# Layer norm by one VectorE instruction per pixel column, and the second stage's loop written out

## The reference, cut to what matters

```python
hidden = einsum('oc,bchw->bohw', w_hidden, x)            # 32 -> 192 channels
hidden = depthwise_3x3(hidden, w_dw)
q, k, v = split(hidden, 3, axis=1)                       # 64 channels each
out = irfft2(rfft2(patches_8x8(q)) * rfft2(patches_8x8(k)))
mu, var = out.mean(axis=1), out.var(axis=1)              # over the 64 channels, per pixel
out_norm = (out - mu) / sqrt(var + 1e-05) * norm_w + norm_b
return einsum('oc,bchw->bohw', w_out, v * out_norm)
x = x + that(group_norm(x))
```

## Time and profile before

| | us |
|---|---|
| median of 3 runs | 2822.24 |
| the profiled execution | 2816.64 |
| its span, first to last instruction | 2814.8 |
| TensorE matmul busy | 2501.0 (89%) |
| TensorE weight load busy | 1660.3 (59%) |
| VectorE busy | 1651.3 (59%) |
| ScalarE busy | 1439.9 (51%) |
| GpSimd busy | 466.5 (17%) |

### The profile page before, as it was taken

How to read it: one execution, slowest core, us unless ns; L and a number is a source line. 1 busy time by engine, 2 the same in 40 slices (tenths; PEclk the granted TensorE clock), 3 DMA queues, 4 the chain that set the end, 5 groups by cost and what they waited for, 6 DMA issues and landing times.

```text
span 2814.8 us, 95766 instructions
## 1 busy us (share of the span) xinstructions
PE 2501.0 (89%) x40199; PEld 1660.3 (59%) x40199; DVE 1651.3 (59%) x4058; ACT 1439.9 (51%) x2381; POOL 466.5 (17%) x322
## 2 busy tenths in 40 slices
PE   7888888699898999898989998999899989999998
PEld 3333333466666666666666666666666666666665
DVE  4666666455555555555555555555555555555565
ACT  3555656555555555554555555545555554455552
POOL 1000000012121212121212121212121212121221
PEclk9988989799999999999999999999999999999999
DMA  6688978622222222222222222222222222222222
GB/s 128 174 228 213 233 203 214 162 59 66 64 64 63 61 61 65 61 60 61 66 62 66 64 67 61 62 61 65 62 66 64 65 62 60 59 62 61 66 56 46
DMA packets 60403, 249.11 MB, mean 88 GB/s; under 512 B 12393, under 2 KB 12658, under 8 KB 53714
## 3 DMA queue, kind: packets, MB, share of 16 engines
q1 hardware_dynamic: 59954, 242.50, 35.2%
HBM read 140.74 MB, written 101.72 MB: 86 GB/s over the span
## 4 chain that ended last, share of the span: by engine, by line
PE 59%; DVE 11%; issue 6%; ACT 3%; DVEq 0%; SPq 0%; ACTq 0%; DMA 0%
PE bank L654 16%; PE bank L577 12%; PE bank L670 9%; PE bank L637 7%; PE bank L590 6%; PE bank L558 6%; PE bank L599 4%; ACT arena L820 3%; DVE arena L1122 2%; DVE arena L1134 2%; DVE arena L1099 2%; DVE arena L1109 2%; DVE arena L1141 2%; DVE arena L1129 1%; ACT arena L865 0%
## 5 line engine op out<-in xcount | busy, mean ns | idle before, releaser
L441 POOL TENSOR_TENSOR arena<-arena 128x8 f32<-128x8 f32 x256 | 442.3, 1728 | 1827.6 <-DVE arena L1115 1817.5
L811 ACT ACTIVATE arena<-bank 100x512 f32<-100x512 f32 x1024 | 614.8, 628 | 227.4 <-PE bank L558 209.8
L577 PE MATMUL bank<-arena 128*64 128x512 f16 x4608 | 711.9, 400 | 7.6 <-issue 4.3
L1199 DVE TENSOR_TENSOR arena<-bank,arena 128x512 f32<-128x512 f32 x512 | 354.3, 692 | 438.4 <-PE bank L654 412.5
L558 PEld LDWEIGHTS bank<-arena 128*36 128x36 f16 (+1 forms) x8192 | 334.1, 106 | 423.2 <-issue 126.9
L558 PE MATMUL bank<-arena 128*36 128x128 f16 (+1 forms) x8192 | 406.7, 224 | 170.3 <-DVE arena L1099 127.2
L654 PE MATMUL bank<-arena 100*64 100x128 f32 x8192 | 510.0, 274 | 7.6 <-DVE arena L1199 7.6
L654 PEld LDWEIGHTS bank<-arena 100*64 100x64 f32 x8192 | 455.7, 136 | 45.4 <-issue 37.3
L512 PE MATMUL bank<-arena 32*32 32x508 f32 (+1 forms) x9216 | 386.8, 654 | 52.6 <-issue 37.7
L820 ACT ACTIVATE arena<-bank,arena 128x256 f32<-128x256 f32 x512 | 261.6, 561 | 172.0 <-PE bank L590 169.4
L1134 DVE TENSOR_TENSOR arena<-arena,bank 128x512 f32<-128x512 f32 x256 | 175.9, 687 | 286.3 <-ACT arena L820 284.8
(11 more groups left out here) (112 smaller groups left out, 1587.0 us busy)
## 6 DMA issues: line engine op xcount, KB each, us to landing
arena<-xn_d SPq DMA_DIRECT2D x128, 536.2 KB, 8.1
xn_d<-arena SPq DMA_DIRECT2D x130, 260.0 KB, 4.5
x_d<-arena SPq DMA_DIRECT2D x64, 512.0 KB, 8.3
arena<-x_d SPq DMA_DIRECT2D x128, 256.0 KB, 4.7
out<-arena SPq DMA_DIRECT2D x128, 256.0 KB, 5.3
arena<-x_in SPq DMA_DIRECT2D x32, 544.0 KB, 9.9
arena<-x_in SPq DMA_DIRECT2D x32, 528.0 KB, 9.7
arena<-spectra_in SPq DMA_DIRECT2D x1, 1152.0 KB
```

The source lines that it names most:

```text
L441: pool.tensor_tensor(tiny["rstd"][:, slot], tiny["var_eps"][:, slot], powers, ALU.pow).then_inc(s_root, 1)
L577: mm = pe.matmul(v_banks[chunk % 3][64 * s:64 * s + 64, :], v_w[:, 64 * tap:64 * tap + 64], at(xs[half], row * WP + 32 * k + dx, [32 * WP, ...
L811: act.activation(h_rows[0:WIN, :, first:first + 4], banks[g % ring][0:WIN, :].rearrange("p (i c) -> p c i", i=4), ACT.Copy).then_inc(s_h_r ...
L1199: dve.tensor_tensor(parts(prod[m % 4][:, 512 * second:512 * second + 512]), parts(k_banks[n % 3]), q_sb[m % 2][:, 256 * second:256 * secon ...
```

## The change

Two things are done.

The first is the layer norm. `centre` and `scale` (one instruction of 512 elements each per piece, the second waiting for the first) and the copy of the means go. `normalise` stands for them: 8 tensor_scalar instructions per piece, one for each pixel column of 64 channels, which subtract the mean and multiply by the root, both read as a scalar per partition, the mean straight from the statistics. With it VectorE's order in `front` changes: a piece is normalised one piece ahead of its gate in place of two, each gate comes one round later in relation to the statistics, and the windows come earlier in relation to the gates.

The second is the loop: on all five engines the loop of the second stage is a Python loop, so all units are written out, with constant waits. The order of the other engines is the same.

```diff
-                dve.tensor_copy(T["pixel_mean"][:, slot], at(T["pixel_stats"], 24 * (p % 4) + 1, [3, 8])).then_inc(s_pixel_mean, 1)
-
-            def centre(u, p):
-                piece = Y4[:, :, :, 4 * p:4 * p + 4]
-                dve.wait_ge(s_pixel_mean, 8 * u + p + 1)
-                dve.tensor_tensor(piece, piece, over(T["pixel_mean"][:, 8 * (p % 4):8 * (p % 4) + 8]), ALU.subtract).then_inc(s_y_centred, 1)
-
-            def scale(u, p):
-                piece = Y4[:, :, :, 4 * p:4 * p + 4]
+
+            def normalise(u, p):
                 dve.wait_ge(s_root, 8 * u + p + 1)
-                dve.wait_ge(s_y_centred, 8 * u + p + 1)
-                slot = slice(8 * (p % 4), 8 * (p % 4) + 8)
-                dve.tensor_tensor(piece, piece, over(T["rstd"][:, slot]), ALU.mult).then_inc(s_y_norm, 1)
+                for s in range(2):
+                    for j in range(4):
+                        pixels = at(Y, 2048 * s + 4 * p + j, [32, 64])
+                        i = 8 * (p % 4) + 4 * s + j
+                        ins = dve.tensor_scalar(pixels, pixels, T["pixel_stats"][:, 3 * i + 1:3 * i + 2], T["rstd"][:, i:i + 1], ALU.subtract, ALU.mult)
+                ins.then_inc(s_y_norm, 1)
...
                     pixel_stats(tail, p)
                     variance(tail, p)
                     if p == 1:
-                        centre(tail, 0)
-                scale(tail, 0)
-                windows()
-                centre(tail, 1)
-                scale(tail, 1)
-                windows()
+                        windows()
                 for p in range(8):
+                    normalise(tail, p)
                     if p < 5:
                         pixel_stats(tail, p + 3)
                         variance(tail, p + 3)
-                    if p < 7 or u is None:
-                        gate(tail, p // 2, p % 2)
-                    if p < 6:
-                        centre(tail, p + 2)
-                        scale(tail, p + 2)
-                    if p in (2, 4, 6):
+                    if p > 0:
+                        gate(tail, (p - 1) // 2, (p - 1) % 2)
+                    if p in (3, 5, 7):
                         residual(tail, p // 2 - 1)
-                    if p > 0:
-                        windows()
+                    windows()
+                if u is None:
+                    gate(tail, 3, 1)
...
-            with dve.Fori(0, NB - 1) as b:
+            for b in range(NB - 1):
                 for half in (1, 0):
```

More of the change, by code:

```diff
@@ L184, in build @@
         s_pixel_stats = semaphore("pixel_stats")
-        s_pixel_mean = semaphore("pixel_mean")
-        s_y_centred = semaphore("y_centred")
         s_var_eps = semaphore("var_eps")
@@ L235, in build @@
         powers = take(8)
-        tiny = {n: take(c) for n, c in (("v_scale", 1), ("v_shift", 1), ("pixel_stats", 96), ("pixel_mean", 32), ("var_eps", 32), ("rstd", 32))}
+        tiny = {n: take(c) for n, c in (("v_scale", 1), ("v_shift", 1), ("pixel_stats", 96), ("var_eps", 32), ("rstd", 32))}
         phases = top[0]
@@ L396, in unit_dma @@
                     load_res(*here)
-            with sp.Fori(0, NB - 1) as b:
+            for b in range(NB - 1):
                 unit_dma(2 * b + 1, (b, 0), (b, 1), (b + 1, 0))
@@ L442, in roots @@
                     pool.wait_ge(s_root, 8 * u + p + 1)
-            with pool.Fori(0, 2 * NB) as u:
+            for u in range(2 * NB):
                 roots(u)
@@ L697, in _ @@
             spectral(0, 0, None)
-            with pe.Fori(0, NB - 1) as b:
+            for b in range(NB - 1):
                 for half in (1, 0):
@@ L870, in _ @@
             act.wait_ge(s_xn_out, 128 * NB)
-            with act.Fori(0, NB - 1) as b:
+            for b in range(NB - 1):
                 for half in (1, 0):
@@ L1087, in _ @@
                 first_stats(later, range(3, NCH))
-            Y4 = Y.rearrange("p (s c j) -> p s c j", s=2, j=32)
-            over = lambda a: a.rearrange("p (s j) -> p s j", s=2).unsqueeze(2).broadcast_to([128, 2, 64, 4])
             def window(u, half, r, b=None):
```

## The result

| | before | after |
|---|---|---|
| median of the runs, us | 2822.64 (4 runs, 2814.06 to 2825.8) | 2867.4 (4 runs, 2851.74 to 2878.0) |
| ratio to before, 95% interval | | 1.0167 (1.0124 to 1.0209) |
| profiled execution, us | 2816.64 | 2866.85 |
| its span, us; mean granted clock | 2814.8; 0.969 | 2865.1; 0.956 |

The change makes the kernel 1.7% slower. I had forecast 2778 us, and at the most 2850.

A forecast was written before the change was run, and what follows sets the result against it. TensorE was taken to bound the kernel, with gaps others set. 31 units gain 53.5 us (loop 32, layer norm 6, clock dips 17); +8 and +2.5 given back leave -43: 2778 us, range 2745 to 2850.

The forecast's parts named there:

- The loop: Second stage written out: 14 turns at 1.17 us removed, 16 us, and constant waits in 30 units, 16 us; 32 together.
- unit 31: Last second-stage unit, already written out behind the loop with constant waits: 69.03 us, taken as base for all 31 units.
- Rival 4: The turn's gap is a refill that straight code has too, and constants give nothing: +32, 2810 us; 5%.
- The price of a piece: VectorE's layer norm: eight columns at 0.224 us, from source line L919, make 1.79 us against 1.48 now.
- Rival 1: A column with a 128-byte stride is read one element a cycle: 0.257 us each, +36, 2814 us; 15%.
- The walk: One unit's events stepped through in the new order: last transpose at 36.7 us against 36.9, 0.2 us won.
- the ring of the windows: Window, hidden group, transpose, ScalarE, gate, window: cut by the new order, so its three waits, 4 us a unit, go.
- I give half back: TensorE's clock dips, 17 us in the second stage, may stay; half is given back, +8 us.
- Rival 3: The clock dips in every unit, as gaps stand closer: +42, 2820 us; 8%.
- rival 2: Small instructions don't overlap: eight columns 2.5 us, VectorE holds up every projection, +105, 2883 us; 19%.
- the two signs that I had named for being wrong: A column costing over 262 ns, or a slower VectorE being late at projections 1 and 2 too.
- The tail: Last tail, with no windows to win, only the dearer piece: 8 x 0.31 = 2.5 us more.

The follow-up runs named there:

- e1: The kernel before with only its five loops written out, layer norm and order untouched: 2810.7 us, ratio 0.9969 to before.
- e2: The changed kernel with its hardware loops kept, so new order and columns alone: 2862.4 us, ratio 1.0157 to before.
- e5: The changed kernel plus ten forms of tensor_scalar, sixteen of each, on scratch behind the last residual: 0.242 us per strided column with two scalars.
- e3: The changed kernel with the two old 512-element operations and the copy of the means in the new order, loops written out: 2782.0 us, ratio 0.9893 to before.
- e11: e1 with 14 matmuls that nobody reads in the 1.85 us wait before the first transpose: 2791.5 us, ratio 0.9900 to before.
- e6: The changed kernel with 22 matmuls that nobody reads in the 2.88 us wait before the first transpose: 2828.5 us, ratio 1.0052 to before.
- e10: The changed kernel with immediates in place of the columns' two scalars, which leaves the layer norm out: 2752.9 us, ratio 0.9760 to before.
- e8: e7's order of VectorE's work with the eight columns for centre and scale, loops written out: 2742.1 us, ratio 0.9745 to before.
- e7: The kernel before with loops written out, two old operations and the author's own VectorE order, windows first: 2640.4 us, ratio 0.9399 to before.

## Why the prediction was wrong, point by point

- **The loop: right in mechanism, too large in sum.** The gap of 2.83 us at the turn is gone, and every undisturbed unit of e1 has the 69.03 of unit 31. But the step "no new fetch is added; at unit 31, in straight code, no gap stands" took one unit for all. Straight code has some six gaps of its own, and the drops of the clock grew. In place of 32 us the old order gave 9. In the new order, where my sum used the same 69.03, it gave nothing of its own (e2). Rival 4, a refill that straight code has too, held half of this: both kinds of gap go with transfers of code. (My parts of the gain, 32, 6 and 17, add up to 55 and not to the 53.5 beside them; over undisturbed units of their kind the dips cost 14.7.)
- **The price of a piece: mis-sized, 1.79 against 1.96 to 2.06.** The step that failed is the one from L919, whose 128 elements lie side by side, to columns with a stride of 128 bytes, at the same rate per element. Rival 1 was right in price, 0.257 forecast, 0.245 to 0.258 measured, and in part in cause: 0.019 of the 0.027 that a column costs over my 0.224 is the stride (e5), and the rest comes only inside the kernel. The argument against it, that the statistics read the same stride at full rate, did not carry over. What I had said of overlap and of writing in place holds.
- **The walk: right in its order of events.** Its waits came where it put them: before transpose 0 2.88 (forecast 2.8), before chunk 3 and before projection 0 up to 0.9 and 1.0 (0.9 and 1.5), and the ring of the windows is cut. At 2.0 us a piece it puts the last transpose at 37.6; the trace has 38.21, 0.6 later, a little more than the half microsecond of error that I gave it. Together with the price this makes the undisturbed unit 1.32 us too short, 41 us, which is nearly the whole gain of 43. With the old operations the new order takes 68.35 a unit (e3).
- **The clock: the step that turned no change into a loss.** "I give half back", +8, is 39 us. The argument for it was that the gaps are as large in sum, and that a slow TensorE is partly hidden where VectorE is late. It counts gaps; e11 and e6 show that the one long wait before the first transpose is what the drops of e1 and of after stand behind. Rival 3 had priced the drops in every unit at +42 and was given 8%, on the ground that 20 units had as much waiting and no drop. That count did not even hold for the same waits: before has one drop behind the wait of 1.85 us, e1 twelve. Nor is it the length alone: behind 1.95 us there are 22 (e10), behind 2.33 also 22 (e8), behind 2.53 there are 17 (e3), behind 2.88 us 24, behind 1.00 none (e7).
- **Rivals are not exclusive.** Rivals 1 and 3 both came true, and a part of 4. Each of them alone ended at 2814 or 2820, no slower than before; rival 1 and rival 3 together add 36 + 42 to 2778, which is 2856, above my range. I had counted them as cases apart. The slower side was given to rival 2 alone, whose cause, no overlap at all, did not come (it needs 0.31 us a column). And neither of the two signs that I had named for being wrong came: a column is under 262 ns, and only projection 0 waits for VectorE (33 waits in 31 units).
- **The tail**: +4.4, forecast +2.5.

**What the parts are worth.** By the medians: the loop written out, -9; the order, -29 on top (e3 against e1); the columns, +85 on top of both. In the sums of the 31 units: -11, -22 and +67. On VectorE a piece costs 2.0 - 1.48 = 0.52 us more, 133 us in 256 pieces, 4.16 us a unit. Of this the undisturbed unit takes over 1.80 us in the new order (70.15 less 68.35) and 2.63 in e7's; the rest of the columns' cost there is mostly the clock. In the old order, in its slowest run, the whole 133 us come back in the sum. VectorE is busy for 63% of the span, and yet its latency ahead of TensorE is passed on by half or more.

**What stays open.** Why of two units with the same waits one loses the clock and the other not, and why the drops stand behind other waits once the loop is written out. Whether the gaps of straight code would go if the data were moved at another time. And how little of the clock's loss would be left if the waits of 0.9 us were filled together with the first.

## What to carry to other kernels

Before many small instructions take the place of a few large ones, price one of them with its own stride and its own operands: the start-to-start distance, not the busy time, and each scalar read from memory by itself. In a unit in which one engine feeds another, look first at which piece the bounding engine waits for and what stands ahead of it in the feeding engine's queue; moving work in that queue gave 6% here with the same instructions, while the change of the instructions lost 3% beside it. And a wait of the bounding engine can cost more than its length, since the work behind it may run at a lower clock; how often that happens could not be read off the kernel before, so give it a range of its own, from no unit to every unit. Add up rivals that can come true together. And when a run gives the number that was expected, look whether its rows show the mechanism too: in e2 they did not.

## What the runs showed of the hardware that I had not expected

- A tensor_scalar of 64 f32 elements costs 0.133 us with two immediates and 0.242 with two scalars from memory, some 0.05 to 0.06 each, beside 0.02 for a stride of 128 bytes (e5).
- Behind a wait of 1.85 us once a unit TensorE's clock fell to half in 12 of 31 units (e1), at some 2 us of longer matmuls each (26 us of excess); work that nobody needs in that wait took 19 us off the time (2810.7 to 2791.5). With a filled wait of 2.88 us (e6) the falls moved to the next waits, two of some 0.9 us, behind which none had stood.
- Straight code of some 2,200 us is not free of gaps: four to six of up to 2.0 us in TensorE's transforms of k, in each kernel written out, each ending 2.6 to 3.0 us behind the start of a transfer of code, and none there in those with a loop of 14 turns, which stand for 2.6 us at each turn instead (36.8 us in 14).
